# The tail behind a selective scan: x times D on GpSimd within the scan, the last sum on VectorE, one norm scale for two, scaled copies mostly on ScalarE

## The reference

```python
def step(h, inp):                      # _L1_attn_ref, n = 16 states
    dA_t, Bu_t, C_t = inp
    h = dA_t * h + Bu_t
    y = jnp.sum(h * C_t[:, None, :], axis=-1)
    return (h, y)
...
return y + x * D_param                 # x is here the layer norm of the residual
...
x = x + _L1_attn_ref(_layernorm(x), ...)
x = x + _L1_ffn_ref(_layernorm(x), ...)
...
# inside _L1_ffn_ref, on its (already normed) x:
h = x + attention(rmsnorm(x, ln1_w), ...)
out = h + moe(rmsnorm(h, ln2_w), ...)
```

## Time and profile before

| | |
|---|---|
| time, median of 3 runs | 2179.1 us (2179.08 to 2182.07) |
| the profiled execution: own time, span | 2183.05 us, 2181.3 us |
| busy: TensorE, VectorE, ScalarE, GpSimd | 87%, 64%, 45%, 35% of the span |
| TensorE clock granted, mean | 0.916 of full speed |

### The profile page before, as it was taken

How to read it: one execution, slowest core, us unless ns; L and a number is a source line. 1 busy time by engine, 2 the same in 40 slices (tenths; PEclk the granted TensorE clock), 3 DMA queues, 4 the chain that set the end, 5 groups by cost and what they waited for, 6 DMA issues and landing times. The chain is left out here.

```text
span 2181.3 us, 27455 instructions
## 1 busy us (share of the span) xinstructions
PE 1892.6 (87%) x9210; PEld 1251.2 (57%) x9210; DVE 1391.5 (64%) x2192; ACT 981.1 (45%) x1684; POOL 768.4 (35%) x1109
## 2 busy tenths in 40 slices
PE   6978664898999898897999899799899999799795
PEld 3446443695448564595447655486446666388442
DVE  4765698464663799475654599576554499666312
ACT  1412773362322795263242598164141398255031
POOL 1146366442210265462120156382120146472201
PEclk9979655997999999998999999999799999899898
DMA  6337100000213176011023076111022257210683
GB/s 242 114 105 242 56 1 0 1 2 20 96 44 116 63 263 215 11 30 41 39 102 102 29 240 223 63 40 35 27 78 100 68 184 264 83 40 21 256 295 104
DMA packets 55024, 221.09 MB, mean 101 GB/s; under 512 B 6240, under 2 KB 6240, under 8 KB 46944
## 3 DMA queue, kind: packets, MB, share of 16 engines
q1 hardware_dynamic: 45728, 195.14, 25.8%
q0 software_dynamic: 5120, 16.78, 2.3%
q10 hardware_dynamic: 4032, 7.34, 0.9%
HBM read 179.65 MB, written 39.58 MB: 101 GB/s over the span
## 5 line engine op out<-in xcount | busy, mean ns | idle before, releaser
L1888 POOL TENSOR_TENSOR Y<-Y,HC 128x1024 f32<-128x1024 f32 x120 | 283.0, 2359 | 218.1 <-DVE HC L1315 218.1
L1304 DVE TENSOR_TENSOR_SCAN HS<-DA,ps 128x1024 f32<-128x1024 f32 x128 | 292.5, 2285 | 23.8 <-PE ps L724 13.5
L1658 ACT ACTIVATE DA<-DL,AB,AN 128x511 f32<-128x511 f32 x256 | 193.8, 807 | 14.8 <-DVE HS L1304 13.5
L932 PE MATMUL ps<-ring,XBT 128*128 128x512 f32 x384 | 189.0, 599 | 0.0
L1762 ACT ACTIVATE PD<-ps,NMX 128x128 f32<-128x128 f32 (+3 forms) x256 | 134.4, 528 | 93.9 <-DVE NMX L1451 89.5
L513 PE MATMUL ps<-ring,XNT 128*128 128x512 f32 x384 | 172.7, 608 | 2.1 <-ACT VA L1605 2.1
L1451 DVE TENSOR_REDUCE NMX<-ps 128x1 f32<-128x128 f32 (+3 forms) x256 | 124.9, 489 | 72.4 <-PE ps L785 71.7
L803 PE MATMUL ps<-V,PTD 128*128 128x33 f32 x1280 | 163.9, 261 | 0.0
L803 PEld LDWEIGHTS ps<-V,PTD 128*128 128x128 f32 x1280 | 162.5, 192 | 0.0
L632 PE MATMUL ps<-XNH,tern 128*128 128x512 f32 x352 | 140.0, 398 | 9.9 <-DVE tern L1204 5.2
L1315 DVE TENSOR_TENSOR HC<-HS,ps 128x1024 f32<-128x1024 f32 x120 | 143.2, 1196 | 0.0
(11 more groups left out here) (233 smaller groups left out, 3968.2 us busy)
## 6 DMA issues: line engine op xcount, KB each, us to landing
ring<-experts_dram SPq DMA_DIRECT2D x48, 1024.0 KB, 5.1
tern<-tern_q SPq DMA_DIRECT2D x33, 768.0 KB, 4.2
ring<-experts_dram SPq DMA_DIRECT2D x48, 512.0 KB, 5.5
RAW<-tern_dram SPq DMA_DIRECT2D x22, 768.0 KB, 5.0
ring<-wqkv_dram SPq DMA_DIRECT2D x4, 3072.0 KB, 10.2
XB<-xg SPq DMA_DIRECT2D x42, 256.0 KB, 3.6
yg<-YB SPq DMA_DIRECT2D x42, 256.0 KB, 4.9
tern_q<-tern SPq DMA_DIRECT2D x11, 768.0 KB, 7.0
```

The lines of the kernel that those rows point to most:

```text
L932: last = pe.matmul(ps[:, g_bank(b)], XBT[:, b % 2, k], weights(b)[:, k * C:(k + 1) * C], start=(k == 0), stop=(k == NK - 1), skip_group_ch ...
L1304: v.tensor_tensor_scan(HS[:, q].rearrange("p j t -> p (j t)"), DA[:, q].rearrange("p j t -> p (j t)"), ps[:, 2 * q:2 * q + 2].rearrange("p ...
L1658: s.activation(DA[:, u % 2, jj, 1:T], DL[:, j, 1:T], ACT.Exp, scale=AN[:, j * NS + n:j * NS + n + 1], bias=AB[:, j * NS + n:j * NS + n + 1 ...
L1888: p.tensor_tensor(y, y, HC[:, q], ALU.add).then_inc(c_y, 1)
```

## The change

- D into x in the scan: behind the sums of half-steps 8, 10, 12 and 14 GpSimd multiplies one channel block of XNT by D in place (128x512), and behind those of half-steps 20 and 22 it adds two blocks of it into Y (128x1024). The four VectorE instructions L1402 are gone.
- The last of the 30 sums (half-step 31, Y blocks 2 and 3) is made by VectorE. TensorE waits for it and for GpSimd's sum of half-step 30.
- The two chained scales become one: rsqrt(var*(1+eps) + eps*eps) in two GpSimd instructions in place of seven. The plain layer norm scale, which phase D's end needs, is made afterwards (`p_base`, two instructions a tile).
- Three of the four scaled copies go to ScalarE (`s_C_end`, four instructions a tile, since its scale is one value for each partition); the fourth stays on VectorE.
- At phase D's end the sum of mean squared and variance is one VectorE instruction in place of two of GpSimd.

```diff
--- before.py
+++ after.py
@@ -97,7 +97,7 @@
           + [(("y", i), "dve") for i in range(NT)]
-          + [(("norm", 3, i), "dve") for i in range(NT)]
+          + [(("norm", 3, i), ("act", "dve")[i == NT - 1]) for i in range(NT)]
           + list(d_transposes())
@@ -725,7 +729,8 @@
         def pe_C_out(pe, experts):
-            pe.wait_ge(c_yt, NK)
+            pe.wait_ge(c_y, 2 * NS - 3)
+            pe.wait_ge(c_yt, 1)
             for i in range(NT):
@@ -742,6 +747,7 @@
         def pe_D(pe, experts):
+            t_emptied(pe, ("norm", 3, NT - 2))
             t_emptied(pe, ("norm", 3, NT - 1))
@@ -1397,10 +1403,9 @@
         def v_C_end(v, experts):
-            for j in range(NK):
-                v.wait_ge(c_y, 2 * NS - 3 + j // 2)
-                v.scalar_tensor_tensor(Y[:, j], XNT[:, j], cst("dpar")[:, j:j + 1], Y[:, j], ALU.mult,
-                                       ALU.add).then_inc(c_yt, 1)
+            v.wait_ge(c_hc, 2 * NS)
+            v.wait_ge(c_y, 2 * NS - 4)
+            v.tensor_tensor(Y[:, 2:4], Y[:, 2:4], HC[:, 1], ALU.add).then_inc(c_yt, 1)
             for i in range(NT + 1):
@@ -1409,8 +1414,7 @@
                     v_normalize(v, 3, i - 1)
-            for i in range(NT):
-                v_evac_scaled(v, 3, i, XNT, cst("ln1"))
+            v_evac_scaled(v, 3, NT - 1, XNT, cst("ln1"))
             if experts:
@@ -1461,6 +1465,7 @@
                 v.wait_ge(stored, 16)
+            v.wait_ge(n_base, NT)
             for i in range(NT):
@@ -1471,6 +1476,9 @@
                     v_stats(v, 4, i, ACC[:, i])
+                    v.wait_ge(n_aggr, 4 * NT + i + 1)
+                    v.scalar_tensor_tensor(RS[:, i, 0:1], MV[:, i, 0:1], MV[:, i, 0:1], MV[:, i, 1:2], ALU.mult,
+                                           ALU.add).then_inc(n_square, 1)
                 if i:
@@ -1735,7 +1743,16 @@
+        def s_C_end(s):
+            for i in range(NT - 1):
+                s.wait_ge(t_full, T_INDEX["norm", 3, i] + 1)
+                for j in range(NK):
+                    ins = s.activation(XNT[:, j, tile(i)], ps[:, T_BANK["norm", 3, i], tile(j)], ACT.Copy,
+                                       scale=cst("ln1")[:, j:j + 1])
+                ins.then_inc(t_free["act"], 1)
         def s_D(s, experts):
+            s_C_end(s)
             s.wait_ge(lat_done, 1)
@@ -1785,7 +1802,7 @@
             p.wait_ge(n_aggr, 4 * k + i + 1)
-            mean, var = MV[:, i, 0:1], MV[:, i, 1:2]
+            var = MV[:, i, 1:2]
             r = [RS[:, i, j:j + 1] for j in range(4)]
@@ -1794,22 +1811,22 @@
             if k == 4:
-                link(p.tensor_tensor(r[0], mean, mean, ALU.mult))
-                link(p.tensor_tensor(r[0], r[0], var, ALU.add))
-                link(p.tensor_scalar(r[0], r[0], RMS_EPS, None, ALU.add))
+                p.wait_ge(n_square, i + 1)
+                link(p.tensor_scalar(r[2], r[0], RMS_EPS, None, ALU.add))
+                p.tensor_tensor(r[1], r[2], half, ALU.pow).then_inc(n_rstd, 1)
+                return
+            if k < 3:
+                link(p.tensor_scalar(r[0], var, LN_EPS, None, ALU.add))
                 p.tensor_tensor(r[1], r[0], half, ALU.pow).then_inc(n_rstd, 1)
                 return
-            link(p.tensor_scalar(r[0], var, LN_EPS, None, ALU.add))
-            if k < 3:
-                p.tensor_tensor(r[1], r[0], half, ALU.pow).then_inc(n_rstd, 1)
-                return
-
-            link(p.tensor_tensor(r[1], r[0], half, ALU.pow))
-            link(p.tensor_tensor(r[2], r[1], r[1], ALU.mult))
-            link(p.tensor_tensor(r[2], r[2], var, ALU.mult))
-            link(p.tensor_scalar(r[2], r[2], RMS_EPS, None, ALU.add))
-            link(p.tensor_tensor(r[2], r[2], half, ALU.pow))
-            p.tensor_tensor(r[3], r[1], r[2], ALU.mult).then_inc(n_rstd, 1)
+            link(p.tensor_scalar(r[2], var, 1.0 + RMS_EPS, LN_EPS * RMS_EPS, ALU.mult, ALU.add))
+            p.tensor_tensor(r[3], r[2], half, ALU.pow).then_inc(n_rstd, 1)
+        def p_base(p, link, i):
+            link(p.tensor_scalar(RS[:, i, 0:1], MV[:, i, 1:2], LN_EPS, None, ALU.add))
+            p.tensor_tensor(RS[:, i, 1:2], RS[:, i, 0:1], HALF[:, 0:1], ALU.pow).then_inc(n_base, 1)
@@ -1879,19 +1896,36 @@
             p_split(p, experts)
-            for u in range(2, 2 * NS):
+            for u in range(2, 2 * NS - 1):
                 q = u % 2
+                y = Y[:, 2 * q:2 * q + 2]
                 p.wait_ge(c_hc, u + 1)
                 if u >= 4:
                     p.wait_ge(c_y, u - 3)
-                y = Y[:, 2 * q:2 * q + 2]
+                if u in (22, 23):
+                    p.wait_ge(c_xy, q + 1)
                 p.tensor_tensor(y, y, HC[:, q], ALU.add).then_inc(c_y, 1)
+                if u in (8, 10, 12, 14):
+                    j = u // 2 - 4
+                    if j == 0:
+                        p.wait_ge(c_u, NK)
+                        p.wait_ge(c_bc, 1)
+                    p.tensor_scalar(XNT[:, j], XNT[:, j], cst("dpar")[:, j:j + 1], None, ALU.mult).then_inc(c_xd, 1)
+                if u in (20, 22):
+                    q = u // 2 - 10
+                    y = Y[:, 2 * q:2 * q + 2]
+                    p.wait_ge(c_xd, 2 * q + 2)
+                    p.wait_ge(c_y, u - 1 - q)
+                    p.tensor_tensor(y, y, XNT[:, 2 * q:2 * q + 2], ALU.add).then_inc(c_xy, 1)
             p.wait_ge(c_ub, NT * (NS + 1))
             p.memset(V1[:, :, :, HD:HD + 1], 1.0).then_inc(ones_set, 1)
         def p_D(p, link, experts):
             for i in range(NT):
                 p_rstd(p, link, 3, i)
+            for i in range(NT):
+                p_base(p, link, i)
             for g in range(NG):
                 for i in range(NT):
                     p_stack(p, g, i)
```

More of the change, by code:

```diff
@@ L331, in build @@
         n_rstd = sem("n_rstd")
+        n_base = sem("n_base")
+        n_square = sem("n_square")
         n_xn = sem("n_xn")
@@ L405, in build @@
         c_y = sem("c_y")
+        c_xd = sem("c_xd")
+        c_xy = sem("c_xy")
         c_yt = sem("c_yt")
```

## The result

| | before | after |
|---|---|---|
| time, median | 2180.6 us (4 runs, 2179.1 to 2184.4) | 2143.4 us (4 runs, 2139.5 to 2144.9) |
| ratio, 95% interval | | 0.9824, 0.9804 to 0.9844 |
| span of the profiled execution | 2181.3 us | 2140.5 us |

The account below looks back on a forecast made before the run. The bound was taken to be the chain hopping between engines behind each scan. Gains of 9.5 + 10.5 + 7.8 + 9.4 = 37.2 plus 4 x 0.3 = 1.2 make 38.4 us: 2179.1 to 2140.7 us, range 2133 to 2149.

Parts of the forecast that it names:

- The sum in Y: Behind the scan: VectorE's sum waits for GpSimd's, TensorE starts 3.5 instead of 7.24 us after S; gain 3.7 us a pass.
- S: Time at which the last two sums into Y start, behind each pass's scan; the forecast counts from it.
- the rival of the unhindered sum: Behind the scan: VectorE's sum runs beside GpSimd's without waiting, 4 x 1.1 us more gained, 2136.3 us; chance 0.10.
- The norms, first pass: Chain behind the scan, no expert products: shorter scale brings the latent projections from S+25.13 to S+15.6; gain 9.5 us.
- D: Time at which TensorE starts the latent projections, behind the norms of each pass.
- P: Time at which the scan's last product ends, S+1.06.
- y: Time at which TensorE starts its transposes of Y behind the scan.
- The norms, passes 2 to 4: Behind the scan: TensorE with four expert products becomes the bound, projections start at S+17.4; gains 10.5, 7.8 and 9.4 us.
- The allowance for the clock: Passes 2 to 4: 0.4 us added because the first expert product falls near the rise of TensorE's clock.
- The rival of the low clock: Passes 2 to 4: TensorE's clock stays low through the first expert product or more, 1.9 x 3 us, 2146.4 us; chance 0.12.
- Hidden work: In the scan: GpSimd's added 11.5 us at most hides beside 54 us idle; `p_base`, about 4 us, ends before D.
- Phase D's end: Last norm of phase D: one GpSimd instruction moves to VectorE, one vanishes; 0.3 us gained a pass, between -0.25 and 0.55.

Follow-up runs that it names:

- the four traces of this stretch: Changed kernel (2143.4 us) and three variants of it: last two sums on VectorE (2143.2), phase-end norm as before (2146.3), more GpSimd scan work (2144.9 us).

## Why the prediction was right

**The sum in Y.** S+3.5 was forecast and S+3.53 measured, gain 3.7 us a pass. The value rested on one row, the 2809 ns of L1402, read as waiting. The experiment with both sums on VectorE shows that reading right: 2341 ns beside GpSimd and 1.22 us without it, so the rival of the unhindered sum (4.4 us more) is out. The rule of the Trainium skill ("SBUF — State Buffer", section "SBUF: two separate sides") agrees with these two numbers. The same page (section "Who interferes with whom") says that a VectorE instruction with at most one SBUF input, outside its faster two-port modes, does not contend with GpSimd; the scan, which took 23 us of added GpSimd work a pass without a change of step, agrees.

**The norms, first pass.** D at S+15.6 forecast, S+15.62 measured; the last XN at y+9.7 forecast, y+9.50 measured. Here the clock is low from P to D in every trace, and the parts undone one at a time add up: 3.7 (Y), 4.6 (scale) and 1.4 us (copies), 9.8 against the 9.5 gained.

**The norms, passes 2 to 4.** TensorE as the bound was right: moving its products takes y to D down to 11.2 us. Two terms of its order were mis-sized, one each way. From the first product's end to D the sum had 7.6 us; measured are 7.0, 6.7 and 6.9, since the four transposes of one tile put only 0.28 us between two products at the high clock (the products of the third pass start at y+6.03 and y+8.18 and take 1.88), where 0.53 was reckoned. The allowance for the clock was too small: up to the first product's end the sum had y+6.3 with its 0.4 us, and y+7.9, 5.8 and 7.5 were measured, as two of the three products took 3.62 us. The rival of the low clock, put at 0.12, thus came true in two passes of three, but not on top of a right sum. By pass D was forecast at S+17.4 and measured at S+18.4, 16.0 and 17.9. The two errors nearly cancel: y+13.9 forecast, mean of the three 13.9, and 13.5 to 13.9 in the four traces of this stretch. This is luck in part; the scatter from pass to pass was not in my sum. Nor does the last XN come at y+9.7 there: 10.90, 9.04 and 10.39, in the second and fourth passes after waiting 1.61 us for TensorE's transposes of the tile two before it. That too is TensorE as the bound.

**Hidden work.** GpSimd's 11 us in the scan (4 x 1.57 + 2 x 2.37) cost nothing that the rows show; doubled, they cost nothing either. `p_base` ends 1.2 us behind D in the first pass and 0.3 in the third, where the forecast had it over before D; in the first pass GpSimd is idle for 16 us behind it, and nobody waits for it.

**Phase D's end.** 0.3 us a pass forecast, 0.33 measured at its place; no time here can tell whether the passes got shorter by it.

**What phase D does with the gain.** I counted it in full. From D to the second latent copy the four passes took 30.7 us before and 31.4 after (the first pass 10.15 instead of 9.05, the second 7.07 instead of 7.46), so 0.7 us was handed back at once. In the first pass that is the clock: it rises 3.8 us behind D before and 6.1 after. The spans differ by 40.8 us, of which 36.6 lie between P and D and 1.3 in phase D's end; the remaining 3 are spread over phases with unchanged instructions, and runs of the same kernel differ by 5 us. The largest piece of the 3 lies between the third pass's second latent copy and the fourth's P, 472.3 us before and 469.1 after. TensorE had the low clock for 41.0 us of it before and for 34.1 after, by the clock's own records in the trace; of all the traces here, those with 34.1 us low took 468.9 to 470.1 us for it, those with 40 or more 470.7 to 472.3. What decides where the clock is low there is open.

**The parts.** Undone one at a time they sum to 13.1 + 14.4 + 3.2 + 1.3 = 32.0 us by the traces, against 37.9 for all. In the first pass nothing is missing, as said above. The missing 6 us lie in passes 2 to 4, where the clock falls differently from trace to trace. The second pass alone lacks 4.8: there the kernel before has the low clock behind its norms and D at y+20.3, while the run with seven instructions escaped it, with D at y+16.2.

## What to carry to other kernels

A wait that shows only as one long instruction among short ones (2809 against 739 ns) is worth as much as one that shows as idle time: look at the maximum of a line's durations, and see what ran on the other engine. Where a chain of small waits is shortened, count anew which engine's order is the next bound before adding up the gain, and whether work that waits for nothing can be moved into that engine's idle time. Work moved to GpSimd under a VectorE loop that reads one operand from PSUM was free here for 23 us of some 54 idle a pass; more was not tried.

## What was not expected of the hardware

An engine order that frees TensorE can lose it again through the clock: with the products moved early the projections took 8.79 us instead of 7.03, as the clock fell when they began. Just ahead of them TensorE had only transposes, with idle times of 0.4, 0.6 and 0.9 us between. That this is the cause is argued; the same order and idle times also gave 7.10 us. And useless matmuls in three gaps shortened P to D by 3.7 us over a run, by what they did to the granted clock.

The clock also sets how far one stretch of unchanged instructions moves: from y to D 12.5 to 14.9 us in passes 2 to 4 of four traces, by whether the clock's rise comes before or behind the first expert product (1.88 us or up to 3.62).
